# Recurrent stage: the first root factor written to PSUM as well, and the transposes of the roots moved between the last two chunks of the feed-forward values

## The reference

```python
r = (xr @ Wr.T); k = (xk @ Wk.T); v = (xv @ Wv.T); g = silu(xg @ Wg.T)
def step(s, rkvw):
    a = k_t[..., :, None] * v_t[..., None, :]
    out = einsum('bhi,bhij->bhj', r_t, u * a + s)
    return a + w_t[..., :, None] * s, out
_, out = lax.scan(step, s0, rkvw)
og = out.reshape(b, l, h, s_)
m = og.mean(-1, keepdims=True)
va = ((og - m) ** 2).mean(-1, keepdims=True)
og = ((og - m) / sqrt(va + 1e-05)).reshape(b, l, e) * gn_w + gn_b
x1 = x + og * g @ Wo.T
...
rr = sigmoid(xr2 @ Wfr.T); kk = square(relu(xk2 @ Wfk.T))
return x1 + rr * (kk @ Wfv.T)
```

## Time and profile before

| | |
|---|---|
| three executions | 3365.83, 3367.73, 3373.61 us |
| the profiled execution | 3371.16 us, its span 3369.4 us |
| recurrent stage, about | 1580 to 2400 us from the span's start |
| steps in which `back` is a sequence, by the starts of L2991 | 16, at 1639.61, 1691.61, 1739.70, 1788.20, ... 2318.36, 2362.37 |
| one step in the loop | 48.3 and 48.5 us in turn |

### The profile page before, as it was taken

The page is one execution under the profiler, slowest core; times in us unless marked ns, Lnnn a source line. Parts: engine busy times, 40 slices in busy tenths (PEclk is TensorE's granted clock), DMA queues, the critical chain, the costliest instruction groups (busy, mean ns, idle before and its releaser), DMA issues. The chain is left out here.

```text
span 3369.4 us, 58824 instructions
## 1 busy us (share of the span) xinstructions
PE 3084.8 (92%) x21440; PEld 2242.8 (67%) x21440; DVE 2092.6 (62%) x3058; ACT 1239.9 (37%) x4419; POOL 908.0 (27%) x645
## 2 busy tenths in 40 slices
PE   8999899979999888986899999997799999899999
PEld 5665566658998855554766777674455555488998
DVE  5555455564434378785899999998254554654543
ACT  3444234422322266661333443342233333322322
POOL 3333233340000012222655555565000000120000
PEclk9999899989999999997899999998899999999999
DMA  4110131100000231111111111110130110101010
GB/s 172 41 44 31 60 147 55 49 32 17 22 25 12 81 148 50 53 34 67 45 40 39 51 51 38 38 48 29 66 136 27 34 45 21 51 20 37 20 37 13
DMA packets 104317, 170.31 MB, mean 51 GB/s; under 512 B 16512, under 2 KB 54016, under 8 KB 100736
## 3 DMA queue, kind: packets, MB, share of 16 engines
q1 hardware_dynamic: 99296, 124.58, 11.6%
q10 hardware_dynamic: 4896, 44.04, 3.3%
HBM read 135.03 MB, written 33.55 MB: 50 GB/s over the span
## 5 line engine op out<-in xcount | busy, mean ns | idle before, releaser
L2641 POOL TENSOR_TENSOR rec_S<-rec_S,rec_r_t 128x1024 f32<-128x1024 f32 x128 | 305.9, 2390 | 317.5 <-DVE rec_S L2966 316.6
L2966 DVE TENSOR_TENSOR_SCAN rec_S<-rec_decay,rec_S 128x1024 f32<-128x1024 f32 x128 | 299.7, 2342 | 8.4 <-DVE rec_S L2951 4.2
L1510 ACT ACTIVATE group_scores<-group_scores,group_negmax 128x128 f32<-128x128 f32 x512 | 197.5, 391 | 29.3 <-DVE group_negmax L1605 19.4
L608 ACT ACTIVATE latent_scores<-latent_scores,region_a 128x256 f32<-128x256 f32 x256 | 126.4, 497 | 71.8 <-DVE region_a L795 71.8
L2087 ACT ACTIVATE mlp_h_t<-mlp_h_t,vectors 128x128 f32<-128x128 f32 x256 | 80.1, 389 | 137.0 <-DVE mlp_h_t L2171 90.2
L2087 ACT ACTIVATE pmlp_h_t<-pmlp_h_t,vectors 128x128 f32<-128x128 f32 x256 | 80.1, 389 | 135.3 <-DVE pmlp_h_t L2171 87.3
L608 ACT ACTIVATE self_scores<-self_scores,self_negmax 128x128 f32<-128x128 f32 x256 | 98.7, 390 | 77.0 <-DVE self_negmax L795 77.0
L608 ACT ACTIVATE cross_scores<-cross_scores,cross_negmax 128x128 f32<-128x128 f32 x256 | 98.7, 389 | 76.4 <-DVE cross_negmax L795 76.4
L3268 PE MATMUL rec_rec_out<-rec_S,head_sum 128*32 128x256 f32 x1024 | 84.0, 401 | 43.7 <-POOL rec_S L2641 42.6
L2951 DVE TENSOR_TENSOR rec_S<-rec_vb,rec_k 128x1016 f32<-128x1016 f32 x96 | 115.3, 1201 | 0.0
L979 PE MATMUL latent_pjA<-latent_src_t,F_query_key 128*128 128x512 f32 x240 | 114.4, 600 | 0.0
(11 more groups left out here) (478 smaller groups left out, 7787.8 us busy)
## 6 DMA issues: line engine op xcount, KB each, us to landing
rec_vb<-v_by_head SPq DMA_DIRECT2D x32, 512.0 KB, 4.1
region_a<-in_C_w ACTq DMA_DIRECT2D x2, 4096.0 KB, 19.1
region_a<-in_G_w ACTq DMA_DIRECT2D x2, 4096.0 KB, 19.5
self_xres<-in_x SPq DMA_DIRECT2D x16, 256.0 KB, 2.6
rows_A<-self_xres SPq DMA_DIRECT2D x16, 256.0 KB, 2.0
cross_ctx_t<-in_ctx_t SPq DMA_DIRECT2D x16, 256.0 KB, 3.4
cross_xres<-rows_A SPq DMA_DIRECT2D x16, 256.0 KB, 2.6
rows_B<-cross_xres SPq DMA_DIRECT2D x16, 256.0 KB, 2.0
```

Of the source, the lines that this page charges most:

```text
L608: nc.scalar.activation(S[:, u, at, :], S[:, u, at, :], ACT.Exp, bias=negmax[:, u, at.start // KB:at.start // KB + 1], accum_out=rowsum[:, ...
L1510: nc.scalar.activation(S[:, u, at, :], S[:, u, at, :], ACT.Exp, bias=negmax[:, u, at:at + 1], accum_out=rowsum[:, u // UPS, sum_column(u, ...
L2641: nc.gpsimd.tensor_tensor(S[u % 4][:, :, :], S[u % 4][:, :, :], bcast(r_t[:, s.k, UNITS[u][0], :], [128, JH, T], 1), ALU.mult)\
L2966: nc.vector.tensor_tensor_scan(St[:, :, :].rearrange(flat), decay[m][:, :, :].rearrange(flat), St[:, :, :].rearrange(flat), 0.0, ALU.mult, ...
```

## The change

Two edits, both in `recurrence_phase`. On DVE, in the first round of the roots, the product `ha` is computed twice, once into a new slice `ha_bank` of bank n (PSUM) and once into `ha` (SBUF) as before, and the instruction after it (L3001 before, L3004 now) reads one input from each. The second round is as it was. On PE, `rstd_t(back)` moves from behind `sum_heads(middle, 1)` to the place between chunks 2 and 3 of `ffn_values(tail, ...)`.

```diff
@@ -2488,6 +2488,7 @@
         hv, ha, hb = (xn2[:, i * NHR:(i + 1) * NHR] for i in range(3))
+        ha_bank = banks.bank("var")[:, 2 * NHR:3 * NHR]
@@ -2996,9 +2997,12 @@
                     dve.wait_ge(root_step, at + 4 * i + 3)
+                    if i == 0:
+                        nc.vector.tensor_tensor(ha_bank, hb, hy, ALU.mult)
                     nc.vector.tensor_tensor(ha, hb, hy, ALU.mult).then_inc(root_step, 1)
                     dve.wait_ge(root_step, at + 4 * i + 4)
-                    nc.vector.scalar_tensor_tensor(hb, ha, -10 / 3, ha, ALU.add, ALU.mult).then_inc(root_step, 1)
+                    nc.vector.scalar_tensor_tensor(hb, ha_bank if i == 0 else ha, -10 / 3, ha, ALU.add, ALU.mult)\
+                        .then_inc(root_step, 1)
@@ -3350,11 +3354,13 @@
                 if tail:
-                    ffn_values(tail, 2, 3)
+                    ffn_values(tail, 2)
+                if back:
+                    rstd_t(back)
+                if tail:
+                    ffn_values(tail, 3)
                 if middle:
                     sum_heads(middle, 1)
-                if back:
-                    rstd_t(back)
```

## The result

The changed kernel takes 3355.71 us, the median of seven runs (3353.73 to 3361.11), against 3368.4 us for seven runs of the kernel before on the same chip (3365.83 to 3373.86). The ratio is 0.9957, with an interval of 0.9948 to 0.9967, that is, 11 to 17 us less; the medians themselves are 12.7 apart. The forecast was 3357.8.

The account below looks back on a forecast made before the run. PE and DVE, both some 95% busy, wait on each other; DVE's path from variance to og_t bounds a step. Ten steps give 5.9, three 2.5, ends 0.9, 0.7 and -0.1: 9.9 off 3367.73, so 3357.8 us; range 3353 to 3368.

Parts of the forecast that it names:

- The wait for POOL: First root round on DVE: with one input in PSUM, L3001 is no longer held by POOL, 0.19 us instead of 1.29.
- Rival (C): First root round: PSUM input does not free the instruction; 0.42 us lost a step, 3373.2 us; chance 0.09.
- The added product: Extra DVE product in the first root round: at most 0.22 us, covered by the wait for POOL.
- The roots and the first stretch of DVE: DVE from the roots to og_t: roots ready and all of DVE 0.90 us earlier; PE newly waits 0.63.
- PE's path to the output product: PE from transpose through chunk 3, head sums and v: reaches the output product 0.63 us later, at 1796.30.
- The output product itself: PE's product after og_t: starts at 1796.30 instead of 1796.89, so 0.59 us gained a step, not 0.90.
- rival (D): PE makes up the 0.3 us counted as lost, by overlap; 13.3 us gained, 3354.4 us; chance 0.06.
- POOL: L2671 held to the end of scan 2, scan 3 held some 0.15 us by multiply 2, at no cost.
- Rival (A): POOL's later chain delays scan 3; a step gains some 0.35 us, 6.0 in all, 3361.7 us; chance 0.14.
- Rival (B): POOL's L2671 and L2659 come ahead of scan 2; 0.74 us lost a step, 3377 us; chance 0.11.
- The ends: Steps outside the thirteen: first gains about 0.9 us, last but one about 0.7, the last loses 0.1.
- The median: Whole kernel: 9.9 us gained in all, set against the earlier median of 3367.73 us, gives 3357.8.

Follow-up runs that it names:

- e2: Against the changed kernel, only the transpose move kept, with both inputs of the first root round read from SBUF again; 3374.21 us, ratio 1.0004.
- e4: Changed kernel with the transpose of the roots ahead of both value chunks; 3372.72 us, ratio 1.0003.
- e1: Against the changed kernel, only the PSUM product on DVE kept, with PE in its old order; 3370.37 us, ratio 0.9995.
- e7: Changed kernel with one head sum before the transpose, PSUM input in both root rounds, and POOL's bonus values ahead of first columns; 3359.02 us, ratio 0.9955.
- e3: Changed kernel with the transpose behind both value chunks, ahead of the head sums; 3366.51 us, ratio 0.9982.
- e9: Changed kernel with all four head sums ahead of the transpose and DVE's gated product ahead of mix 0; 3364.74 us, ratio 0.9974.
- e10: e9 plus POOL's bonus values ahead of the first columns and PSUM input in both root rounds; 3360.89 us, ratio 0.9966.
- e11: Changed kernel with the transpose ahead of the decay and mix products and both chunks; one execution, 3409.42 us.

## Why the prediction was right, and where it was off

**The wait for POOL.** Right. Predicted for the freed instruction: 0.19; measured: 0.191 to 0.192 in sixteen cases, and the second round held to 0.29, ending at 1782.83 behind POOL's 1782.78. The Trainium skill, SBUF — State Buffer, in its section on the ports, has the shared pair held for a whole instruction by whoever starts first. L2672, held to the end of its scan, the scans held by POOL's wide products and the power that came second agree with it. The power that came first does not: by the rule the scan of 2181.21 would be held to the power's end at 2181.73, and it lost 0.02. The measurement decides: a power of one column does not hold a scan for its recorded length. Rival (C) falls. The page VectorE: DVE Perf Modes, section on the errata, in the Trainium skill, gives PSUM sources more fixed cycles than SBUF sources; the rows show none of it at 32 columns (0.19 either way). My estimate from it also charged two bank accesses, though its table is for sources and one of the two is an output.

**The added product.** Counted as at most 0.22, measured 0.11: L3002 starts 0.10 behind L3001, since nothing between them waits. It changed nothing, as the wait covers it.

**The roots and the first stretch of DVE.** Right to 0.01: the transposes at 2.57 of the step (predicted 2.57), L3015 at 2.93 (2.93), so 0.90 sooner than before. PE's wait, 0.46 for a predicted 0.63, is the same: the profile counts it from chunk 2's recorded end, I had counted it from when chunk 3 could have started.

**PE's path to the output product.** This is the step that was off. The forecast was "PE thus comes to the output product at 1795.67 + 0.63 = 1796.30", which is 8.10 of the step, and it came at 7.93. Chunk 3 stands at 2.73 (2.77), the head sums at 3.69 (3.73) and v at 4.25 (4.30): some 0.04 less, behind the transposes. Then v to the output product is 3.67 to 3.68, where I had taken the modelled end of v in a step that ends in a wait, 3.80. A recorded end is not when the next instruction can start. Where PE had something to do at once, it started 0.13 sooner than that end says.

**The output product itself.** I took 1.91 for its four instructions on both sides. With no wait ahead of them they take 1.82 (1788.57 to 1790.38; e2 and e4 show the same, e1 with its wait 1.91). The wait is not the whole rule: four such instructions also take 1.91 where PE comes to them busy, behind the 64-row products of `decay_and_mix` (1789.19 to 1791.10 in the earlier trace rows). What they cost depends on what stands ahead of them, here v. The two terms together are some 0.26: in the ten steps of the loop the measured 0.87 is 0.59 + 0.04 + 0.13 + 0.09 and 0.02 unaccounted; in the other three it is 0.92, where I had 0.85. This is rival (D), "PE makes up the 0.3 that I call lost, by overlap at the new places", to which I had given 0.06 with the words that little speaks for it. PE's rows do repeat to 0.03 us, but only where it comes to an instruction in the same way: behind the same one, and with or without a wait. The steps alone give 11.4 us, where the forecast's thirteen gave 8.4.

**POOL.** Right, point by point. L2672 lasts 1.98 under scan 2 (predicted to its end), scan 3 is held by 0.17 (predicted some 0.15), and that costs nothing (e7). Rival (A) falls. Rival (B) did not occur, but e3 shows its mechanism. Its price is not tested there: in e3 chunk 3, and with it POOL, comes 0.8 earlier than (B) has it, so the 0.79 a step lost against the changed kernel is no measure of the 0.74 that I had worked out against the kernel before (0.72 by its own rows: scan 2 at 1793.36 for 1792.64). The margin in the changed kernel is 0.30 us, L2672 at 1784.48 against scan 2 at 1784.18; I had worked out 0.33.

**The ends.** The first step gave 2.2 in place of 0.9, and the traces say from where. The output product stands 9.58 behind the first root, against 10.28, which puts DVE's residual 0.78 sooner: this is what I had counted, as 0.9. The scan that follows it stood at 18.34, behind a wait of 0.61 for POOL's `inputs`, and stands at 16.88 without a wait, since POOL's chain hangs on scan 3, which is 1.67 sooner: 0.68 more, a wait that I had not looked for. The last 0.74 are TensorE's clock. PE in the kernel before, then in the changed one, and the window over it in the kernel before:

```profile
1671.08 5.44 PE L3152 MATMUL rec_bank_d<-rec_f_in,region_a 128*128 128x128 f32 x32 [1.79 <-DVE rec_f_in L3035]
```

```profile
1666.02 3.81 PE L3156 MATMUL rec_bank_d<-rec_f_in,region_a 128*128 128x128 f32 x32 [1.33 <-DVE rec_f_in L3039]
```

```profile
1671.08:1676.50 5.42, 5.42 (x36) 5.30 (x40) 5.38 (x8) 3.38 (x9) 2.37 (x1) 0.69 0.00 0
```

Behind a wait of 1.79 us the granted clock was 0.69 there, and DVE waited 0.85 for PE at the end of the step. e1 has the same wait at a clock of 1.00 (3.81 for the same instructions) and a first step of 50.09. So these 0.74 are not sure to come with the change: e1, e9 and e10 have that wait in the first step too, and none of them lost the clock there. The last but one step gave 1.0 for 0.7. Behind it 0.7 went back where I had written 0.1, but all later stages are in this number.

**The median.** The sum of 9.9 went with a median of 3367.73 to 3357.8. The truth, 3355.71, is inside the range and in the direction of (D), because some 14 us were the change's in the profiled pair, and 3.6 us more of that pair lie ahead of the first root and are no effect of it. That the forecast is only 2.1 us off is in part luck: the medians differ by 12.7, 2.8 more than the sum of 9.9, and the kernel before, at 3368.4 over seven executions, is 0.7 above the 3367.73 that I started from.

## What to carry to other kernels

When two engines wait on each other in turn, freeing one shows nothing until the other's order is made to fit: either edit was worth nothing alone (0.9995 and 1.0004), and both together 0.9957. Before moving an instruction onto a stretch shared by VectorE and GpSimd, list which instructions there read two SBUF tensors, and in which order they arrive; a few hundredths of a microsecond decide whether one of them waits for a whole other one (0.06 behind the scan: 2.57; 0.01 ahead of it: 0.53). When costing a move on TensorE, measure from start to start and not to the recorded end, and take the price of an instruction from rows in which the same one stands ahead of it, with a wait or without as in the new order.

## What the runs showed of the hardware

- In the thirteen steps TensorE's granted clock stayed at 1.00 behind waits for the roots of 0.46 us (the change) and 1.35 (e2), fell behind waits of 1.50 (e4) in four, and behind waits of 2.59 (e11) in all. The chunks behind it then took 2.8 to 3.7 us in place of 1.88. So a wait can cost more than its length, and the length alone does not decide: of eight waits of 1.78 or 1.79 us ahead of the same product (L3152 with rec_f_in) the clock fell behind three (one in the kernel before, two in e10) and not behind five (e1, e9 and e10). In the first step, where PE waited 3.42 us for the roots in the changed kernel, v took 5.39 (5.10 in the kernel before, behind waits of 3.04 and 1.11), in place of the 3.84 of a step in the loop.
- One of the four head sums by itself took 0.55 us to the next instruction, all four together 0.57.
- Two VectorE products of 32 columns with no semaphore between them start 0.10 apart, with one between them 0.22.
- A power on GpSimd (0.54 us) that started 0.01 us ahead of a scan (2181.20 and 2181.21 in e10) was not held, and the scan took 2.31 for 2.29; one that came 0.06 behind a scan lasted 2.57.
- Four 128 x 512 instructions take PE 1.82 us to the next start directly behind v; 1.91 behind v and a wait of 1.2 us; and 1.91 with no wait behind the products of `decay_and_mix`, in all thirteen steps of the kernel before.
